# Layer 2's feed-forward and layer 3's attention in a four-layer decoder: another plan of steps

## The reference

```python
# layer 2, feed-forward (128 -> 512 -> 128), both weights and both inputs quantised
h = layernorm(x, ln1_w, ln1_b)            # x is already normalised once
h = bitlinear(h, w1, b1)                  # int8-like rows times ternary weights
h = gelu(h, approximate=False)
h = layernorm(h, ln2_w, ln2_b)            # 512 wide
x = x + bitlinear(h, w2, b2)
# layer 3, attention: 16 heads of 64
q, k, v = (split_heads(norm(x) @ W + b) for W, b in ...)
prob = softmax over keys of (q k^T / 8);  x = x + concat(prob v) @ Wo + bo
# layer 3, cross-attention: softmax over the 16 heads of one token, head against head,
# layer norm, output projection
```

## Time and profile before

| | |
|---|---|
| median of 3 runs | 1099.58 us (1098.29 to 1102.47) |
| profiled execution | 1095.55 us |
| its span (first to last instruction) | 1093.7 us |
| PE busy | 815.3 us (75% of the span) |
| DVE busy | 611.6 us (56%) |
| ACT busy | 349.3 us (32%) |
| POOL busy | 316.2 us (29%) |
| mean granted PE clock | 0.861 of full |

### The profile page before, as it was taken

The page is one execution under the profiler, slowest core; times in us unless marked ns, Lnnn a source line. Parts: engine busy times, 40 slices in busy tenths (PEclk is TensorE's granted clock), DMA queues, the critical chain, the costliest instruction groups (busy, mean ns, idle before and its releaser), DMA issues. The chain is left out here.

```text
span 1093.7 us, 15967 instructions
## 1 busy us (share of the span) xinstructions
PE 815.3 (75%) x5969; PEld 591.4 (54%) x5969; DVE 611.6 (56%) x1414; ACT 349.3 (32%) x683; POOL 316.2 (29%) x318
## 2 busy tenths in 40 slices
PE   4974797892686275688877755999999996167994
PEld 2542453581353164567645433677777686144994
DVE  2654872323669962886666787764345545843222
ACT  1110474331121111245535541444342332011331
POOL 1354200203238723332221211000053433415232
PEclk9985798896688676999989886999999998558897
DMA  9302200361000003544473000000000000005685
GB/s 370 148 2 86 70 7 1 93 189 36 20 1 1 0 1 73 111 92 85 112 203 88 3 1 1 2 1 2 1 2 1 2 1 1 0 1 184 211 285 161
DMA packets 44678, 72.44 MB, mean 66 GB/s; under 512 B 4817, under 2 KB 36737, under 8 KB 43033
## 3 DMA queue, kind: packets, MB, share of 16 engines
q1 hardware_dynamic: 38921, 65.72, 20.4%
q0 software_dynamic: 1728, 3.59, 1.0%
q10 hardware_dynamic: 3952, 2.10, 0.7%
HBM read 58.65 MB, written 15.89 MB: 68 GB/s over the span
## 5 line engine op out<-in xcount | busy, mean ns | idle before, releaser
L847 DVE TENSOR_REDUCE space<-PS 128x2 f32<-128x512 f32 x128 | 83.2, 686 | 40.1 <-PE PS L651 39.7
L2544 DVE TENSOR_REDUCE space<-PS 128x2 f32<-128x512 f32 x64 | 43.3, 689 | 83.0 <-PE PS L2242 82.8
L831 ACT ACTIVATE annex<-PS 128x384 f32<-128x384 f32 (+1 forms) x128 | 67.2, 544 | 57.9 <-PE PS L662 29.2
L2279 PEld LDWEIGHTS PS<-space 128*128 128x128 f32 x512 | 61.2, 191 | 16.8 <-issue 16.5
L2279 PE MATMUL PS<-space 128*128 128x65 f32 x512 | 68.6, 280 | 0.0
L2259 PE MATMUL PS<-space 64*128 64x256 f32 x256 | 67.1, 403 | 0.2 <-ACT space L2362 0.2
L1947 POOL TENSOR_TENSOR space<-space 128x1536 f32<-128x1536 f32 x16 | 54.6, 3435 | 32.7 <-ACT space L1820 26.4
L2242 PE MATMUL PS<-space 64*128 64x256 f32 x256 | 62.7, 401 | 0.1
L1170 PE MATMUL PS<-space 128*128 128x128 f32 x444 | 58.2, 287 | 4.2 <-ACT space L1239 2.3
L1305 DVE TENSOR_TENSOR space<-PS,space 128x512 f32<-128x512 f32 (+1 forms) x28 | 19.2, 687 | 74.3 <-ACT space L1232 69.2
L1170 PEld LDWEIGHTS PS<-space 128*128 128x128 f32 x444 | 54.4, 200 | 6.8 <-issue 3.8
(11 more groups left out here) (492 smaller groups left out, 2196.3 us busy)
## 6 DMA issues: line engine op xcount, KB each, us to landing
space<-in_e_l_ffn SPq DMA_DIRECT2D x22, 768.0 KB, 4.6
space<-in_e_l_ffn SPq DMA_DIRECT2D x23, 192.0 KB, 3.0
l_ffn_sorted<-in_slots SPq DMA_DIRECT2D x2, 1584.0 KB, 25.6
space<-l_attn_scratch_k SPq DMA_DIRECT2D x8, 384.0 KB
space<-l_ffn_sorted SPq DMA_DIRECT2D x10, 264.0 KB, 4.2
weights<-in_w_l_xattn SPq DMA_DIRECT2D x1, 2504.0 KB, 15.2
weights<-in_w_l_attn SPq DMA_DIRECT2D x1, 2124.0 KB, 12.0
space<-l_xattn_scratch_q SPq DMA_DIRECT2D x4, 512.0 KB, 3.4
```

Of the source, the lines that this page charges most:

```text
L831: nc.scalar.activation(P[:, u % 8, 0:keys], PS[:, 3 + u % 2, 0:keys], ACT.Exp).then_inc(exp_done, 1)
L847: nc.vector.tensor_reduce(m[:, :, at_h], max_bank(u).rearrange("p (c k) -> p c k", c=2), AX_X, ALU.max).then_inc(max_done, 1)
L2279: last = nc.tensor.matmul(out, p[:, 256 * kc + 128 * qc:256 * kc + 128 * qc + 128], VB[:, b % 2, kc, h, :], start=kc == 0, stop=kc == 1)
L2544: nc.vector.tensor_reduce(MX[:, b % 2, :, h], PS[:, max_bank[a], :].rearrange("p (c k) -> p c k", c=2), AX_X, ALU.max).then_inc(max_done, 1)
```

## The change

`SHIFT` goes from 176 to 170. `PLAN` has other steps: sequences 0 and 1 keep negative steps for most of their pieces, sequences 2 and 3 begin in steps 1 and 18. The order in which jobs are placed is another: the feed-forward's jobs first, then q and k, whose wished step is now the later of one behind T and three before their first use, then v, and the output projection (t, o) last, with o at least one step behind its t. The wished steps for t and v are as before. No instruction is added or taken away. The whole diff:

```diff
--- before.py
+++ after.py
@@ -454,7 +454,7 @@
 UNITS = B * HEADS
 LAG = HEADS + 8
 WIDE = 64
-SHIFT = 176
+SHIFT = 170
 
 
 def split_parts(engine, own, parts, rest, full):
@@ -2014,10 +2014,10 @@
         "_multiplied", "_summed", "_maxed", "_shifted", "_exped", "_dens", "_summed2", "_scaled"))
 
     SHARED = {B - 2: 0, B - 1: 3}
-    PLAN = {"in": (-58, -42, -24, -9), "twice": (-54, -38, -20, -6), "norm1": (-50, -34, -16, -2), "quant1": (-49, -33, -11, -1),
-            "f1": (-43, -26, -6, 4), "f2": (-36, -23, -3, 7), "gelu": (-33, -21, -2, 8), "hidden": (-29, -17, 1, 11), "norm2": (-24, -12, 4, 14),
-            "affine2": (-23, -11, 5, 15), "quant2": (-22, -9, 6, 16), "f3": (-14, -4, 10, 20), "f4": (-11, -1, 12, 22), "attn": (-9, 0, 13, 23),
-            "normed": (-6, 2, 15, 25), "T": (-3, 4, 17, 27)}
+    PLAN = {"in": (-52, -30, 1, 18), "twice": (-49, -26, 3, 20), "norm1": (-46, -21, 5, 21), "quant1": (-45, -20, 6, 23),
+            "f1": (-38, -16, 8, 25), "f2": (-32, -13, 10, 27), "gelu": (-30, -11, 11, 28), "hidden": (-27, -8, 12, 29), "norm2": (-24, -6, 13, 30),
+            "affine2": (-23, -5, 14, 31), "quant2": (-22, -4, 15, 32), "f3": (-17, 0, 17, 34), "f4": (-15, 2, 18, 35), "attn": (-14, 3, 19, 36),
+            "normed": (-12, 4, 20, 37), "T": (-6, 6, 21, 38)}
     assert all(PLAN["in"][b] + shift > before.out_at(b) for b in range(B))
     LEAD, DELAY, ALONE = HEADS // 2, 13, 43
 
@@ -2054,10 +2054,6 @@
 
     for b in range(B):
         place(first_at(16 * b + 15) + (3 if b < B - 1 else 1), "M", b, 0)
-    for b in range(B):
-        for i in range(6):
-            place(second_at(16 * b + 15) + (3, 3, 4, 4, 5, 6)[i], ("t", "t", "o")[i % 3], b, i)
-    first_x = [job_at["o", b, 5] for b in range(B)]
     f = place(PLAN["f1"][0], "w", 0, 0)
     piece(f + 1, "weights", 0)
     place(-20, "b", 0, 0)
@@ -2072,11 +2068,23 @@
                 late = f - steps[b]
             else:
                 piece(f, what, b)
+    for b in range(B):
         for i in range(4):
-            place(max(f + 1, 16 * b - 18) + 2 * i, "q", b, i)
-            place(max(f + 1, 16 * b - 18) + 2 * i, "k", b, i)
+            f = max(job_at["T", b, 0] + 1 + i, first_at(16 * b + 4 * i) - 3)
+            place(f, "q", b, i)
+            place(f, "k", b, i)
+    for b in range(B):
         for i in range(4):
             place(second_at(16 * b) - 6 + i, "v", b, i)
+    for b in range(B):
+        for i in range(6):
+            f = second_at(16 * b + 15) + (3, 3, 4, 4, 5, 6)[i]
+            if i % 3 < 2:
+                place(f, "t", b, i)
+            else:
+                place(max(f, job_at["t", b, i - 1] + 1), "o", b, i)
+    first_x = [job_at["o", b, 5] for b in range(B)]
+    for b in range(B):
         f = first_x[b]
         piece(f, "cross", b)
         place(f - 2, "xk", b, 0)
```

## The result

| | before | changed |
|---|---|---|
| median | 1099.45 us (4 runs, 1098.29 to 1102.47) | 1125.83 us (4 runs, 1119.70 to 1132.87) |
| ratio | | 1.0237, interval 1.0204 to 1.0271 |
| profiled execution, span | 1095.55, 1093.7 us | 1119.70, 1117.9 us |

Forecast were 1111.5 us and a range up to 1120: the direction is right, the size is not. Five further rounds on another chip gave medians of 1120.55 us (1104.09 to 1126.61) against 1101.06 (1092.02 to 1117.07), 19.5 us apart. Ratios, here 1.011 (1.003 to 1.019), leave out executions over 1.5% above the fastest of their kernel (three of these six, three of the 17 of the kernel before, and the traces of the second run of the changed kernel and of "The order only" are of such ones), while medians are of all.

The account below looks back on a forecast made before the run. It took VectorE's in-order feed-forward queue to bound the gap before layer 3, and TensorE the attention behind it. Its terms summed to +11.9 us: 1107.5 profiled, 1111.5 on the median's scale, range 1096 to 1120.

Parts of the forecast that it names:

- Term 1: Gap before layer 3's first unit: T directly behind layer 2's last output product, which stays put; -15.4 us.
- Term 2: Steps 0 to 13, first unit to second pass: PE waits for banks and inputs from DVE; +11.4 us.
- The bank rule: Opening: k and v jobs take banks that DVE must first empty; k waits put at 2.1 and 2.9 us.
- Term 3: Behind step 13: k, q and feed-forward work formerly done before the second pass lands where PE is full; +3.2 us.
- Term 4: Later feed-forward steps: f4 follows f3 by one step, twice, waiting about 0.75 each; +1.4 us.
- Term 5: Last sequence's maxima: their splitting is held behind GpSimd's two products, so M waits 8.1 us, not 1.5; +6.6 us.
- the memsets: Last maxima: by three earlier GpSimd memsets, the first splitting operation is held until both products end, at 11.3.
- the reading I had put beside it: Last maxima: exclusive lock; first splitting operation slips in at 6.8, the next meets the second product; again near +6.6.
- Term 7: Cross-attention 1 two steps later: second pass starts 1.7 late, output transpose adds 0.5; +2.2 us.
- Term 6: Steps behind the last maxima: the longer wait leaves 5 us of PE work at half speed; +2.5 us.
- Rival 4: Clock lost in the opening too, 7 us more, 1118.5 us; chance 0.12.

Follow-up runs that it names:

- The order only: Kernel before with only the new placing order of jobs, its SHIFT 176 and step table kept; 1129.06 us, ratio 1.0206.
- shift_back: Changed kernel with four auxiliary banks in the opening and GpSimd's products behind the splitting of the last maxima, SHIFT back at 176; 1103.02 us, ratio 1.0027.
- filled_waits: Changed kernel with 45 unused TensorE products put into the waits of seven opening steps; 1114.61 us, ratio 1.0136.
- split_first: Changed kernel, GpSimd's two products of sequence 1 also waiting until VectorE has split the last sequence's maxima; 1101.13 us, ratio 1.002.
- banks_split_filled: Changed kernel with four opening banks, GpSimd's products behind the maxima splitting, and 22 unused products in remaining waits; 1094.99 us, ratio 0.9933.
- four_banks_split_first: Changed kernel with four auxiliary banks in the opening and GpSimd's products of sequence 1 behind the splitting of the last maxima; 1098.37 us, ratio 0.9985.
- before_held: Kernel before with one added wait: GpSimd's products of sequence 1 start only when the last maximum but one is done; 1111.36 us, ratio 1.0105.
- longer distances with filled waits: Changed kernel with four banks, splitting before GpSimd's products, several jobs moved to later steps, 19 unused products in remaining waits; 1087.56 us, ratio 0.9887.
- four_banks: Changed kernel with idle banks 5 and 6 joining 7 and 2 for auxiliary jobs of steps -1 to 12; 1107.87 us, ratio 1.004.
- changed kernel again: Changed kernel unaltered, run again for a second trace; 1120.55 us, ratio 1.011.

## Why the prediction was wrong, step by step

- **Term 1, first unit, -15.4:** -15.5 (24.0 to 8.5 us). T stands directly behind the last output product, and 8.3 us later comes the first unit. But the output product did not stay where it was: the changed plan reaches it 1.9 us earlier, so the term is -17.4 in all. Of the 15.5 the table makes 11.2 and SHIFT 4.3 (shift_back).
- **Term 2, opening, +11.4** (its own 42.9 - 31.6 is 11.3)**:** +11.3 at full clock (42.9 us, filled_waits), +12.9 in two traces (44.5). The bank rule was the cause, as argued: four banks take 10.3 us off.
- **Term 3, work moved, +3.2:** PE's busy time behind the opening goes from 145.72 to 148.93 us in split_first, +3.2.
- **Term 4, later waits, +1.4:** too low. Idle time of PE in that stretch goes from 4.3 to 8.4 us (150.0 - 145.72, 157.3 - 148.93): +4.1. I had counted f4 behind f3 (0.75 twice, as forecast) and left out f3 of sequence 2 behind its quantising (1.40), T of 2 behind its centring (0.94) and xT of 0 behind its own (1.32).
- **Term 5, the hold, +6.6:** +6.2 (3.2 to 9.4 us); M waits 7.70 where 8.1 was forecast. The size is right and the way is not the one that I drew from the memsets: the first operation is not held until both products are done, it ends with the first of them, and the second operation is held by the second product. That is the reading I had put beside it, by which the sum is the same.
- **Term 7, +2.2:** nothing of it is there. At full clock the second passes are 40.5 us against 41.6, but that 1.1 is no gain: eight products fewer stand in this stretch (345 for 353) and eight more behind it (825 for 817).
- **Term 6, the clock, +2.5, "bounds 0 and +8", with nothing for the opening: this step failed.** The clock took 8.8 + 1.3 = 10.1 us in the first trace (opening, second passes) and 1.6 + 1.4 + 9.0 = 12.0 in the second (opening, main stretch, second passes). I put in 2.5 and wrote of the waits of term 2 "as DVE is behind there anyway, I put nothing". In fact DVE is busy for only 23.6 of the 51.7 us of the opening and idle for 28, so there was nothing to hide a slow PE behind: with the waits filled the same opening takes 42.9 us.

What the sum would have been: without the clock my terms give +9.4. Measured without it they are -17.4 + 11.3 + 3.2 + 4.1 + 6.2 - 1.1 = +6.3; so terms 1 and 7 were too high, term 4 too low, and their errors partly cancel, which is luck. With 10.1 to 12.0 us of clock it is +16.4 to +18.3. Rival 4 had both places, 7 us in the opening on top of 2.5 behind M, and with its +18.9 it is what happened; I gave it 0.12.

The +16.4 to +18.3 fits the 19.5 between all executions of the second comparison. It does not reach the 26.4 of the first: with every term as measured the forecast would have been 1116 to 1118 us, inside the stated range, where 1125.83 was measured. Of that comparison's trace (+24.2) 5.0 us lie ahead of the first altered piece, inside the 14 us by which that point scatters in the kernel before, and 2.8 behind the second passes. Why four executions on that chip all were so slow stays open.

Of the Trainium skill, "TensorE: Matmul & The Clock Gate" (what is actually happening) says that throttled is the default and activity releases it. By it I had called the upper bound as likely as zero, and then took a value near zero. The runs agree on the falls of the opening: its clock is 0.80 to 0.95 in the nine traces in which a wait of 2 us or more is left in it, and 1.00 in filled_waits and in banks_split_filled. They don't agree on the release: 27.5 us of unbroken work at half clock (four_banks_split_first) are activity that released nothing for that long. "SBUF — State Buffer" (the shared port pair) says that the pair is an exclusive lock for a whole instruction. The held operations agree with it in the traces of the changed kernel and of before_held, each ending with the product that it met.

## What to carry to other kernels

Price a new wait on a PE-bound path twice: its length, and what it can do to the clock behind it. Here 8 us of waiting cost up to 9 us more, and the second part comes and goes from run to run, so that one trace shows it in one place and the next in another; two traces of each kernel are the least for such a sum. When a plan is moved, look first at what each job takes over from its predecessor (a bank) and at long operations of GpSimd beside short ones of VectorE on the critical path: a bank rotation and one ordering wait turned this change from 1.1% to 2.4% slower into no difference (ratio 0.9985), and longer distances with filled waits into 1.1% faster. And before a wait is moved or filled, look up in the plan which job it belongs to: two kinds of job on one source line cost me edits at a place where nothing waited.

## What the hardware showed that I had not expected

- How long PE stays at half clock after a fall is not set by the wait: after the same 7.7 us wait 1.3, 3.2 and 9.0 us were lost in three traces (changed kernel, four_banks, changed kernel again), after the same 1.41 us wait nothing or 10.7.
- A fall may follow a wait as short as 1.31 us (filled_waits, near 795 us).
- Products whose results nobody uses, put in the place of waits, kept the opening at full clock in the two kernels in which no wait of 2 us was left in it (filled_waits, banks_split_filled). The medians fell by 3.4 us in one pair (1098.37 to 1094.99) and 5.8 in another (1093.37 to 1087.56), each pair on two chips and with overlapping intervals.
- A wait that looks like VectorE's load can be a bank's: with four banks VectorE did the same 23.7 us of work in 34.2 us that had taken 44.5.
